# Decoder block on one Trainium2 core: where and in what pieces three layer-norm statistics are taken, the term order of the first two projections, and the spacing of the feed-forward transposes

## The chip, the cores and the metric

The kernel runs on one core of one Trainium2 chip. The metric is the device time of one execution in microseconds, the median of several. The engines are PE (TensorE, matmuls and transposes), DVE (VectorE), ACT (ScalarE), POOL (GpSimd) and SP (SyncE, which only issues transfers). Each works through its own list of instructions in order, and they wait for each other by semaphores.

## The reference: what is computed

`x` and `ctx` have 4 batches of 512 tokens by 512 features. Cut to what matters:

```
x = x + attn(layernorm(x), q_w, q_b, k_w, k_b, v_w, v_b, o_w, o_b)   # causal, 16 heads of 32
x = x + xattn(layernorm(x), ctx, ctx)                                # causal, 16 heads, no weights
h = layernorm(x)
x = x + relu(h @ W_up.T) @ W_down.T + sum(top-2 softmax of h @ W_gate.T) * (h @ W_expert)
```

Each layer norm takes mean and variance over the 512 features of a token, so there are three of them for each batch: before self-attention, before cross-attention and before the feed-forward.

## The kernel before, in words

**Work in steps and slots.** Both attentions are cut into 64 pairs of heads (32 groups of 4 heads). `ORDER` puts them in a row: 14 groups of self-attention, then `cscscc`, then 12 of cross-attention, so the groups 14, 16, 18, 19 are the four cross groups of batch 0, and 20 to 23, 24 to 27, 28 to 31 those of batches 1 to 3. A step `s` is one pair, and a slot `i` (0 to 7) is one of its 2 heads by 4 query blocks; `z = 8 * s + i`. I write slot 31.1 for step 31, slot 1. All engines walk the same steps, each with its own list.

**What a slot holds.** PE (loop at L652) does the scores of pair s+1 for slot i (`scores`, L466), then a quarter of a filler job, then the transposes of the probabilities of pair s (`turn`, L480). At slot 0 of even steps it also does probabilities times values of the group that ended (`values`, L513, called pv below), and at slot 1 of odd steps ahead of a cross group the queries' transposes (`queries`, L617). Scores have 3 PSUM banks: those of slot i wait until DVE is through the slot three before (L464). DVE (loop at L858) reduces the scores to a row maximum and moves them to `probs` (`top_of`, L682), copies the turned blocks 2, 3, 6, 7 (`turned`, L692), and takes reciprocals (L696), low halves of split operands (L768, L777, L804), the residual behind the output projection (L784), statistics (`ln_stats` L709 and L711, `f_stats_of` L716 and L718) and norms (L737, L745). ACT does the exponentials (L910), the other copies of turned blocks (L919) and the high halves. POOL scales the probabilities of self-attention (`scaled`, L1023, once DVE's reciprocal is there), adds a cross group's output to the residual (`added`, L1066, in step 2G+3 of group G), splits the keys (`keys`, L1056 and L1058) and the feed-forward weights (`f_split`, L1081 and L1083), and turns variances into reciprocal deviations (`ln_scale` L1034, `f_scale` L1040).

**Fillers.** `plan()` (L136) gives each projection its slots and one of two PSUM banks (`m_bank`): Q, K, V, the output projection O, and for the feed-forward of batch f from slot `feed_start(f)` = 344, 408, 472, 536: FL (4 transposes of the normed input, at u+1, u+2, u+4, u+5; the third waits until ACT and DVE have emptied the bank of the first), FG (gate), FU, FE, FD (up, expert, down). `plan()` also gives turns a free filler bank where one stands idle for long enough. Most projections are made of three products (`three`, L517): low times high, high times low, high times high, for each of 4 chunks of the contraction.

**Statistics before.** `stats_slots(j)`: j = 1 to 3 are the self-attention norms of batches 1 to 3. j = 4 to 7 are the cross-attention norms of batches 0 to 3: at slots 168, 169, 176, 177 (step 21 and 22), 256, 256, 272, 272 (steps 32 and 34), 339 to 342 (step 42), and 384, 384, 385, 385 (step 48). Batches 0 to 2 are read from the copy that SP loads back from memory (`load_x`, at steps 20, 30 and 40); batch 3 is read from `xres`. `f_stats_slots(f)`: slots 1, 2, 4, 5 of steps 41, 49, 57, 65, one token block of 512 features in each, after all four cross groups of the batch have been added.

**Start.** The first transposes go into `m0`, `m1`, `pv` and `t0`. The first projections Q0 and K0 run chunk by chunk, so their first product waits for the first low half (L750).

The statistics of before are

```python
            def f_stats_of(f, t):
                if t == 0:
                    dve.wait_ge(c_out, KC * (f + 1))
                nc.vector.bn_stats(f_stats[:, t, :], RES[f][:, t, :]).then_inc(f_stat, 1)
                dve.wait_ge(f_stat, NT * f + t + 1)
                nc.vector.bn_aggr(f_mv[:, t, :], f_stats[:, t, :]).then_inc(f_mv_done, 1)
```

and POOL's add, on which they wait, is the last thing but the scale factors in its step:

```python
                if s % 2 == 1 and other((s - 3) // 2):
                    added((s - 3) // 2)
```

## Time and profile before

| | |
|---|---|
| median of 3 runs | 714.7 us (713.9 to 716.91) |
| the profiled execution | 711.97 us, of which the span of its instructions is 710.0 us |
| PE busy | 674.7 us, 95% of the span |
| DVE, ACT, POOL busy | 70%, 71%, 36% |
| mean granted clock of TensorE | 0.995 |
| chain of work that ended last | PE 80%, DVE 7%, ACT 6% |

The profile is one execution; its own time is 711.97 us, 2.7 us under the median of the runs. A time in the trace is counted from the start of its span. A row of the timeline gives the start, the duration, the engine, the line, the operation with output and inputs, how many such instructions it merges, and in brackets how long the engine was idle just before and what released it. The granted clock is a share of 2.4 GHz, so 0.5 is 1.2 GHz.

### The profile page before, as it was taken

To read this page: it belongs to the slowest core of one execution; us is meant where nothing else is said; L and a number is where in the kernel's file an instruction comes from. 1 tells how busy PE (TensorE), PEld (TensorE's weight loads), DVE (VectorE), ACT (ScalarE), POOL (GpSimd) and SP (SyncE) were. 2 spreads that over 40 slices of the span, in tenths; PEclk is the share of its full clock that TensorE was granted. 3 is DMA by queue.
4 is the path that set the end of the run, shared out by engine and by line. 5 is a ranking of instruction groups with operands and counts; after the bars stand their busy time and mean duration, and the time that the engine had idled before them with its cause. 6 is when DMAs were issued, how large, how long until landed. Compare 5 with 4: busy or idle time off the path is not lost.

```text
span 710.0 us, 13884 instructions
## 1 busy us (share of the span) xinstructions
PE 674.7 (95%) x4488; PEld 523.8 (74%) x4488; DVE 494.6 (70%) x1730; ACT 501.4 (71%) x1450; POOL 256.9 (36%) x391
## 2 busy tenths in 40 slices
PE   7998999999999999999889987999989999899998
PEld 6777777777787777777666755777768777677786
DVE  6568766766766776776878788767887669664632
ACT  5678877777876778787899887776588667874110
POOL 4745644333555335742564415333112102000100
PEclk9999999999999999999999999999999999999999
DMA  9763533336423573445946584633463443510101
GB/s 313 186 155 75 141 70 90 82 94 185 116 61 90 124 212 84 102 105 146 275 122 168 153 236 121 166 95 97 96 183 89 111 101 87 163 38 1 59 1 59
DMA packets 52327, 86.12 MB, mean 121 GB/s; under 512 B 8609, under 2 KB 16801, under 8 KB 52257
## 3 DMA queue, kind: packets, MB, share of 16 engines
q1 hardware_dynamic: 52256, 85.25, 46.1%
q8 instruction: 36, 0.59, 0.3%
q14 instruction: 35, 0.28, 0.1%
HBM read 27.55 MB, written 7.34 MB: 49 GB/s over the span
## 4 chain that ended last, share of the span: by engine, by line
PE 80%; DVE 7%; ACT 6%; issue 2%; DMA 2%; POOL 2%; SPq 1%; POOLq 0%; ACTq 0%; DVEq 0%
PE t L480 16%; PE m L519 14%; PE m L520 14%; PE m L521 14%; PE pv L513 9%; PE s L466 8%; DVE probs L682 3%; ACT probs L910 3%; ACT prob L919 1%; PE m L585 1%; DVE prob L692 1%; DMA stack<-stage 1%; POOL probs L1023 1%; PE m L480 1%; PE m L534 1%
## 5 line engine op out<-in xcount | busy, mean ns | idle before, releaser
L682 DVE CUSTOM_DVE_ANT_0 probs<-s,mask 128x128 f32<-128x128 f32 (+3 forms) x512 | 246.6, 483 | 130.7 <-PE s L466 129.0
L910 ACT ACTIVATE probs<-probs,negmax 128x128 f32<-128x128 f32 (+3 forms) x512 | 284.5, 559 | 46.1 <-DVE negmax L682 45.2
L480 PE MATMUL t<-ident,probs 128*128 128x128 f32 x1140 | 203.5, 277 | 11.4 <-ACT prob L919 6.5
L466 PE MATMUL s<-stack 96*128 96x128 f32 (+3 forms) x512 | 197.8, 394 | 5.5 <-DVE negmax L682 2.8
L1023 POOL TENSOR_SCALAR probs<-probs,rsum 128x128 f32<-128x128 f32 (+3 forms) x256 | 133.4, 539 | 176.9 <-DVE rsum L696 176.6
L919 ACT ACTIVATE prob<-t 128x384 f32<-128x384 f32 (+1 forms) x231 | 124.7, 540 | 97.7 <-PE t L480 96.7
L480 PEld LDWEIGHTS t<-ident,probs 128*128 128x128 f32 x1140 | 144.7, 141 | 60.6 <-ACT prob L919 10.5
L466 PEld LDWEIGHTS s<-stack 96*128 96x128 f32 x512 | 97.9, 191 | 18.7 <-DVE negmax L682 4.1
L910 ACT ACTIVATION_READ_ACCUMULATOR probs<-probs,negmax 128x1 f32 x512 | 98.9, 193 | 0.0
L692 DVE COPY prob<-t 128x256 f32<-128x256 f32 (+1 forms) x218 | 77.1, 354 | 30.9 <-PE t L480 29.9
L519 PE MATMUL m<-xT_hi,w_lo 128*128 128x512 f32 x192 | 78.3, 408 | 1.2 <-DVE xT_lo L750 1.2
L520 PE MATMUL m<-xT_lo,w_hi 128*128 128x512 f32 x192 | 75.7, 394 | 0.0
L521 PE MATMUL m<-xT_hi,w_hi 128*128 128x512 f32 x192 | 75.5, 393 | 0.0
L519 PE MATMUL m<-w_hi,xT_lo 128*128 128x512 f32 x128 | 52.7, 412 | 0.0
L520 PE MATMUL m<-w_lo,xT_hi 128*128 128x512 f32 x128 | 50.4, 394 | 0.0
L521 PE MATMUL m<-w_hi,xT_hi 128*128 128x512 f32 x128 | 50.2, 392 | 0.0
L682 DVE DVE_READ_ACCUMULATOR2_ANT negmax<- 128x1 f32 x512 | 42.5, 83 | 0.0
L521 PEld LDWEIGHTS m<-xT_hi,w_hi 128*128 128x128 f32 x192 | 36.1, 188 | 8.6
L513 PE MATMUL pv<-prob,cv 128*32 128x128 f32 (+3 forms) x512 | 38.0, 436 | 1.5 <-ACT prob L919 1.4
L519 PEld LDWEIGHTS m<-xT_hi,w_lo 128*128 128x128 f32 x192 | 36.7, 191 | 2.8 <-DVE xT_lo L750 1.4
L520 PEld LDWEIGHTS m<-xT_lo,w_hi 128*128 128x128 f32 x192 | 36.5, 190 | 2.9
L513 PE MATMUL pv<-prob,V 128*32 128x128 f32 (+3 forms) x512 | 37.8, 435 | 0.1
(144 smaller groups left out, 946.2 us busy)
## 6 DMA issues: line engine op xcount, KB each, us to landing
stack<-stage SPq DMA_DIRECT2D x384, 128.0 KB, 2.3
xt<-in_x SPq DMA_DIRECT2D x16, 256.0 KB, 4.7
xres<-in_x SPq DMA_DIRECT2D x4, 1024.0 KB, 6.1
kraw<-in_ctxT SPq DMA_DIRECT2D x16, 256.0 KB, 3.0
cv<-in_ctx SPq DMA_DIRECT2D x16, 256.0 KB, 3.1
x<-xres SPq DMA_DIRECT2D x3, 1024.0 KB, 5.5
res<-x SPq DMA_DIRECT2D x8, 256.0 KB, 6.4
out<-res SPq DMA_DIRECT2D x2, 1024.0 KB, 4.8
```

The source lines that it names most:

```text
L466: nc.tensor.matmul(score_tile(P, i), stack[0:RS, P % 2, h, 0, chunk(qb)], stack[0:RS, P % 2, h, 1, 0:N], start=True, stop=True).then_inc(s ...
L480: mm = nc.tensor.transpose(dst[:, chunk(qb - kb)], probs[:, (2 * P + h) % 3, OFF[qb] + PART * kb:OFF[qb] + PART * kb + PART], ident[:, :])
L513: mm = nc.tensor.matmul(pv_bank[HD * j:HD * j + HD, PART * kb:T], v[:, HD * j:HD * j + HD], prob[kb][:, j, :], start=(kb == 0), stop=(kb = ...
L519: nc.tensor.matmul(dst, lhs[1], rhs[0], start=(c == 0), stop=False)
L520: nc.tensor.matmul(dst, lhs[0], rhs[1], start=False, stop=False)
L521: return nc.tensor.matmul(dst, lhs[0], rhs[0], start=False, stop=(c == KC - 1))
L534: mm = nc.tensor.transpose(dst[:, chunk(t)], src[:, t, chunk(c)], ident[:, :])
L682: nc.vector.tensor_tensor_reduce(probs[:, (2 * P + h) % 3, OFF[qb]:OFF[qb + 1]], score_tile(P, i), mask[:, T - N:T], -SCALE, BIG, ALU.add, ...
L692: nc.vector.tensor_copy(prob[kb][:, 2 * (P % 2) + h, :], turned_tile(P, i)).then_inc(t_dve, 1)
L910: nc.scalar.activation(tile, tile, ACT.Exp, bias=negmax[:, P % 2, h, qb:qb + 1], scale=-1.0, accum_out=total).then_inc(p_exp, 1)
L919: nc.scalar.activation(prob[kb][:, 2 * (P % 2) + h, :], turned_tile(P, i), ACT.Copy).then_inc(t_act, 1)
L1023: nc.gpsimd.tensor_scalar(tile, tile, rsum[:, P % 2, h, qb:qb + 1], 0.0, ALU.mult, ALU.add).then_inc(p_done, 1)
```

## The change

It does five things.

1. The statistics of cross-attention for batches 0 to 2 are taken from `xres`, one slot after the output projection's residual of the same token block is there (steps 10 to 12, 18 to 20, and 25, 28, 29, 30), with their own buffers for each batch and their own scale step on POOL (`c_scale`, steps 12, 20, 30, 48). The norm itself stays where it was, and now waits for the loaded copy. SP waits for these statistics before it overwrites `xres`. Batch 3 keeps its slots.
2. The statistics of the feed-forward are taken for each cross group when it has been added: in slots 1, 2, 4, 5 of step 2G+3 of every cross group G (steps 31, 35, 39, 41, 43, 45 and so on to 65), 128 features for each of 4 token blocks, so 64 narrow statistics in place of 16 wide ones; behind the fourth group they are aggregated.
3. Q0 and K0 do the four products of high parts first, and the others behind them.
4. The first transposes go into the three score banks and `pv`.
5. The third and fourth transposes of FL move one slot back (u+5 and u+6), for batches 0 to 2.

```diff
-def stats_slots(j):
+def o_start(b, t):
+    if b == B - 1:
+        return PAIRS * (SELF_END + min(t, 2)) + 4 * (t // 3)
+    if b == B - 2:
+        return PAIRS * (25, 28, 29, 29)[t] + 4 * (t // 3)
+    return PAIRS * (PAIRS * (b + 1) + 1 + t) + (4, 4, 0, 1)[t]
...
+def c_stats_slots(b):
+    z = PAIRS * PAIRS * (2 * B - 2)
+    return [z, z, z + 1, z + 1] if b == B - 1 else [o_start(b, t) + NT + 1 for t in range(NT)]
...
-def f_stats_slots(f):
-    z = PAIRS * (PAIRS * (f + B + 1) + 1)
+def f_stats_slots(G):
+    z = PAIRS * (2 * G + 3)
     return [z + 1, z + 2, z + 4, z + 5]
...
             if f < B - 1:
-                put(("FL", f, m), 0, u + 1 + m + m // 2, 1, 1)
+                put(("FL", f, m), 0, u + 1 + m + 2 * (m // 2), 1, 1)
...
-        first_bank = [*m_bank, pv_bank, t_bank[0]]
+        first_bank = [*s_bank, pv_bank]
...
                     sp.wait_ge(x2_stored[b - 1], 16)
+                    sp.wait_ge(c_mv_done, NT * b)
                     sp.dma_start(xres[:, :, :], x_in[b]).then_inc(res_loaded, 16)
...
+            def first_three(dst, w, k):
+                late = ([("lo", c) for c in (0, 1)] + [("x", c) for c in range(KC)] + [("lo", c) for c in (2, 3)] if w == WQ else
+                        [("x", c) for c in range(KC)] + [("lo", c) for c in range(KC)])
+                terms = [("hi", c) for c in range(KC)] + late
+                for n in range(3 * k, 3 * k + 3):
...
+            def c_stats_of(b, t):
+                dve.wait_ge(o_out, NT * b + t + 1)
+                nc.vector.bn_stats(c_stats[:, t, :], xres[:, t, :]).then_inc(c_stat, 1)
+                dve.wait_ge(c_stat, NT * b + t + 1)
+                nc.vector.bn_aggr(c_mv[:, b, t, :], c_stats[:, t, :]).then_inc(c_mv_done, 1)
+            def f_stats_of(G, t):
+                n = RANK[G]
+                f = n // KC
+                dve.wait_ge(c_out, n + 1)
+                nc.vector.bn_stats(f_stats[:, t, n % KC, :], RES[f][:, t, chunk(n % KC)]).then_inc(f_stat, 1)
+                if n % KC == KC - 1:
+                    dve.wait_ge(f_stat, NT * n + t + 1)
+                    nc.vector.bn_aggr(f_mv[:, t, :], f_stats[:, t, :, :].rearrange("p c s -> p (c s)")).then_inc(f_mv_done, 1)
...
+            def c_norm(b, t):
+                if t == 0:
+                    dve.wait_ge(c_rstd_done, b + 1)
...
+                if b < B - 1:
+                    dve.wait_ge(x_loaded[t], 16 * (B + b + 1))
...
+                for j in range(B):
+                    if s == c_stats_slots(j)[-1] // PAIRS:
+                        c_scale(j)
                 for f in range(B):
-                    if s == f_stats_slots(f)[-1] // PAIRS:
+                    if s == f_stats_slots(CROSS_AT[KC * f + KC - 1])[-1] // PAIRS:
                         f_scale(f)
```

## Rows read from the trace of the kernel before

**Rows 1.** The page, part 1: busy time and share of the span.

```profile
PE 674.7 (95%) x4488; PEld 523.8 (74%) x4488; DVE 494.6 (70%) x1730; ACT 501.4 (71%) x1450; POOL 256.9 (36%) x391
```

**Rows 2.** Groups by line, DVE: busy us, mean ns of one; idle before.

```profile
L709 DVE BATCH_NORM_STATS2 stats<-xt 128x6 f32<-128x512 f32 x20 | 13.6, 679 | 4.3 <-DMA xt<-in_x 4.3
...
L711 DVE BATCH_NORM_AGGREGATE mv<-stats 128x2 f32<-128x6 f32 x32 | 5.8, 182 | 1.1
```

**Rows 3.** Busy time in stretches of 10 us: PE, PEld, DVE, ACT, POOL, clock, DMA.

```profile
200.00:210.00 10.00, 10.00 (x59) 8.29 (x58) 7.21 (x29) 8.04 (x23) 6.59 (x11) 1.00 0.35 80
...
430.00:440.00 10.00, 6.22 (x38) 4.90 (x37) 8.44 (x31) 7.96 (x27) 4.39 (x6) 0.91 0.58 146
```

**Rows 4.** Timeline, the start: the last high half, Q0's first and twelfth product.

```profile
12.07 0.62 ACT L979 ACTIVATE xT_hi<-t 128x512 fp32r<-128x512 f32 x1
...
12.15 0.47 PE L519 MATMUL m<-xT_hi,w_lo 128*128 128x512 f32 x1 [1.24 <-DVE xT_lo L750]
...
14.77 0.39 PE L521 MATMUL m<-xT_hi,w_hi 128*128 128x512 f32 x1
```

**Rows 5.** Timeline of step 31, DVE, POOL and PE.

```profile
342.98 0.18 DVE L696 RECIPROCAL rsum<-rowsum 128x4 f32<-128x4 f32 x1
...
343.25 2.06 POOL L1023 TENSOR_SCALAR probs<-probs,rsum 128x128 f32<-128x128 f32 x4 [1.66 <-DVE rsum L696]
...
343.56 0.56 DVE L682 CUSTOM_DVE_ANT_0 probs<-s,mask 128x384 f32<-128x384 f32 x1 [0.41 <-PE s L466]
...
345.28 1.28 POOL L1066 TENSOR_TENSOR xt<-cn,xt 128x512 f32<-128x512 f32 x1
...
345.76 0.36 PE L466 MATMUL s<-stack 96*128 96x256 f32 x1
...
347.64 2.36 PE L513 MATMUL pv<-prob,V 128*32 128x512 f32 x32
```

**Rows 6.** Timeline of step 35, DVE, POOL and PE.

```profile
373.83 0.56 DVE L682 CUSTOM_DVE_ANT_0 probs<-s,mask 128x384 f32<-128x384 f32 x1 [0.42 <-PE s L466]
...
375.68 1.28 POOL L1066 TENSOR_TENSOR xt<-cn,xt 128x512 f32<-128x512 f32 x1
...
376.61 0.69 DVE L804 TENSOR_TENSOR stage<-pv,stage 128x512 fp32r<-128x512 f32 x1
...
377.40 2.36 PE L513 MATMUL pv<-prob,V 128*32 128x512 f32 x32
```

**Rows 7.** Timeline of steps 41 to 43, PE and POOL.

```profile
425.35 0.33 PE L466 MATMUL s<-stack 96*128 96x128 f32 x1 [1.03 <-DMA stack<-stage]
...
431.22 1.28 POOL L1058 TENSOR_TENSOR stage<-kraw,stage 128x512 fp32r<-128x512 f32 x1
...
437.33 0.23 POOL L1034 TENSOR_SCALAR veps<-mv 128x4 f32<-128x4 f32 x1 [4.84 <-DVE mv L711]
...
438.08 0.90 PE L480 MATMUL t<-ident,probs 128*128 128x128 f32 x3 [1.11 <-DVE prob L692]
...
438.65 0.61 POOL L1081 CAST w_hi<-V 128x512 fp32r<-128x512 f32 x1
...
442.49 1.27 POOL L1066 TENSOR_TENSOR res<-cn,res 128x512 f32<-128x512 f32 x1
...
443.36 0.66 PE L534 MATMUL m<-ident,f_xln 128*128 128x128 f32 x4 [1.42 <-DVE xT_lo L768]
...
447.78 2.36 PE L513 MATMUL pv<-prob,cv 128*32 128x512 f32 x32
```

**Rows 8.** Timeline of step 51, PE: FL's third transposes, the next pv.

```profile
525.59 0.66 PE L534 MATMUL m<-ident,f_xln 128*128 128x128 f32 x4 [1.51 <-DVE xT_lo L768]
...
530.00 2.36 PE L513 MATMUL pv<-prob,cv 128*32 128x512 f32 x32
```

**Rows 9.** Timeline at the end of step 11, PE and DVE.

```profile
151.90 2.36 PE L513 MATMUL pv<-prob,V 128*32 128x512 f32 x32
...
153.17 0.29 DVE L692 COPY prob<-t 128x128 f32<-128x128 f32 x1
```

More of the change, by code:

```diff
@@ L273, in decoder_block @@
         rstd = sb("rstd", [PART, NT])
-        f_stats = sb("f_stats", [PART, NT, 6])
+        c_stats = sb("c_stats", [PART, NT, 6])
+        c_mv = sb("c_mv", [PART, B, NT, 2])
+        c_veps = sb("c_veps", [PART, B, NT])
+        c_rstd = sb("c_rstd", [PART, B, NT])
+        f_stats = sb("f_stats", [PART, NT, KC, 6])
         f_mv = sb("f_mv", [PART, NT, 2])
@@ L521, in three @@
                 return nc.tensor.matmul(dst, lhs[0], rhs[0], start=False, stop=(c == KC - 1))
+            def first_three(dst, w, k):
[3 more added lines that the diff above has]
+                for n in range(3 * k, 3 * k + 3):
+                    term, c = terms[n]
+                    if term == "hi":
+                        pe.wait_ge(w_hi_done[w], c + 1)
+                        pe.wait_ge(lnt_hi, c + 1)
+                    elif term == "x":
+                        pe.wait_ge(lnt_lo, c + 1)
+                    elif w == WQ and c >= 2:
+                        pe.wait_ge(wq_rest, c - 1)
+                    else:
+                        pe.wait_ge(w_lo_done[w], c + 1)
+                    weight = w_lo if term == "lo" else w_hi
+                    mm = nc.tensor.matmul(dst, weight[:, w, c, chunk(0)], (xT_lo if term == "x" else xT_hi)[:, c, :],
+                                          start=(n == 0), stop=(n == 3 * KC - 1))
+                return mm
             def bank_for(key):
@@ L549, in fill @@
                     w = WQ if kind == "Q" else WK
-                    if n == 0 and kind == "Q" and c >= 2:
-                        pe.wait_ge(wq_rest, c - 1)
-                    elif n == 0:
-                        pe.wait_ge(w_lo_done[w], c + 1)
-                    if kind == "Q" and n % KC == 0:
-                        pe.wait_ge(lnt_lo, KC * (n // KC) + c + 1)
-                    mm = three(dst, (w_hi[:, w, c, chunk(n % KC)], w_lo[:, w, c, chunk(n % KC)]),
-                               (xT_hi[:, c, :], xT_lo[:, c, :]), c)
+                    if kind == "Q" and n and n % KC == 0:
+                        pe.wait_ge(lnt_lo, KC * (n // KC) + c + 1)
+                    if n == 0:
+                        mm = first_three(dst, w, c)
+                    else:
+                        mm = three(dst, (w_hi[:, w, c, chunk(n % KC)], w_lo[:, w, c, chunk(n % KC)]),
+                                   (xT_hi[:, c, :], xT_lo[:, c, :]), c)
                     if c == KC - 1:
@@ L883, in _ @@
                         back_scaled(s // 2 - 1)
-                    for j in range(1, 2 * B):
+                    for j in range(1, B):
                         for t in range(NT):
@@ L887, in _ @@
                                 ln_stats(j, t)
+                    for j in range(B):
+                        for t in range(NT):
+                            if z == c_stats_slots(j)[t]:
+                                c_stats_of(j, t)
+                    for j in range(1, 2 * B):
                         for t in range(NT):
                             if z == norm_slots(j)[t]:
-                                ln_norm(j, t)
+                                ln_norm(j, t) if j < B else c_norm(j - B, t)
+                    for G in CROSS_AT:
+                        for t in range(NT):
+                            if z == f_stats_slots(G)[t]:
+                                f_stats_of(G, t)
                     for f in range(B):
-                        for t in range(NT):
-                            if z == f_stats_slots(f)[t]:
-                                f_stats_of(f, t)
                         for t in range(NT):
@@ L1122, in _ @@
                     added((s - 3) // 2)
-                for j in range(1, 2 * B):
+                for j in range(1, B):
                     if s == stats_slots(j)[-1] // PAIRS:
                         ln_scale(j)
+                for j in range(B):
+                    if s == c_stats_slots(j)[-1] // PAIRS:
+                        c_scale(j)
                 for f in range(B):
-                    if s == f_stats_slots(f)[-1] // PAIRS:
+                    if s == f_stats_slots(CROSS_AT[KC * f + KC - 1])[-1] // PAIRS:
                         f_scale(f)
```

65 lines of the change are left out of this document (25 added, 40 removed).

## The prediction

> **What bounds the kernel now.** I read the page's busy times first. PE is busy for 674.7 of 710.0 us [rows 1], so only some 35 us can be had by removing waits, and work moved to another engine helps only where PE stands idle for it. The busy time by stretch says where that is. From 200 to 210 us PE is busy throughout while DVE has 2.8 us to spare; from 430 to 440 us PE is busy for 6.22 us, DVE for 8.44, and the granted clock is 0.91 [rows 3], so for some 1.8 us of it PE ran at 1.2 GHz instead of 2.4. Then I read the timeline there and at the steps in which the change puts a new wait. So the sum is made at six places: the start, the new statistics under a full PE, steps 31 and 35, steps 41 to 43, and steps 51 and 59.
>
> **Start: -0.2 us.** Q0's first product starts at 12.15 us, behind 1.24 us of waiting for a low half [rows 4]. Products of high parts can start about 1 us earlier, but the fourth of them needs the last high half, which ends at 12.69 (12.07 + 0.62) [rows 4], and 9 of the 12 products are then still to start. The twelfth starts at 14.77, so they follow each other at (14.77 - 12.15) / 11 = 0.24 us, and 0.23 without the slower first one: 12.75 + 8 x 0.23 = 14.59 for the last start, against 14.77 [rows 4]. What follows (stage, transfer, first scores) is a chain behind it and moves along. Bounds: 0 and -1.2, the whole wait; I take the value that is worked out.
>
> **Cross statistics behind the output projection: +1.0 us.** 12 statistics of 0.68 us with 12 aggregates of 0.18 [rows 2], some 0.8 each as they overlap, move to steps 10 to 30. There PE is full and DVE is not [rows 3], so most cost nothing: the cover is DVE's idle time. Gone, it would cost up to 12 x 0.86 = 10 us. One slot in each batch is tight: in step 11 DVE takes the new one (slot 5) with two low halves of transposes beside it, and its last copy of the step ends at 153.46, while pv, begun at 151.90, needs that copy for its last tenth, 0.9 x 2.36 = 2.1 us after its start, at 154.0 [rows 9]. 0.8 us more is 0.3 us too late. I count 0.3 for each of batches 0 and 1 and 0.4 for batch 2, whose steps 28 and 29 look the same. Range 0 to 2.4. What the old places give back: steps 21, 22 nothing (PE full); steps 32 and 34 nothing, since DVE did them in the shadow of a pv of 2.36 us [rows 5] and waited for the next scores behind them. SP's new wait and POOL's moved scale factors (two small instructions, the first 0.23 us [rows 7]) are met before they are due; in step 30 POOL has 1.66 us free ahead of 343.25 [rows 5], enough. Only step 42 gives something, below.
>
> **The feed-forward statistics, step 31: +3.0 us.** This is the new wait. In slot 31.1 DVE now waits for group 14 to be added. POOL does that add behind four scalings that wait for DVE's reciprocal of the same slot: reciprocal at 342.98, scalings 343.25 to 345.31, add 345.28 to 346.56 [rows 5]. DVE has nothing to do in between, as its list is in order; behind the wait stand all its maxima and copies. With a narrow statistic at 0.29, the price of DVE's 128-wide copy [rows 9] (bounds: 0.17, a quarter of a wide one, and 0.68, a whole one [rows 2]), the next maximum starts at 346.9 instead of 343.56, 3.3 us late. PE may run three slots of scores ahead: its scores of 32.5 were issued at 345.76 and need this maximum, so PE stops there. Before the next pv DVE has to do two more narrow statistics (0.6) and has some 0.9 us of its own old waits (0.41 of them in the row of 343.56) to absorb them: 3.3 + 0.6 - 0.9 = 3.0, pv at 350.6 instead of 347.64 [rows 5]. Nothing gives it back, as ACT has work without a pause from there to step 34. Bounds: 1.5 (about the wait from 345.76 to the end of that maximum, 346.9 + 0.56 - 0.1 = 347.4, alone) and 4.7 (see the clock, next).
>
> The clock could add to this. The row first: in the one stretch of 10 us in which PE stood idle for 3.8 us, in pieces of at most 1.11 us [rows 7], the granted clock was 0.91 [rows 3], that is 0.09 x 10 / 0.5 = 1.8 us at 1.2 GHz; so short waits, close together, have lowered it in this kernel. The Trainium skill has a rule that speaks against new waits of this kind: "TensorE: Matmul & The Clock Gate", section on psum-queue depth-cycling, says that PE idling briefly between groups of matmuls makes the clock oscillate, and that what is lost between the bursts is the price; the trace agrees. By the rule each of steps 31 and 35 would carry a slow spell and the sum would be 3.4 us more. I leave it out of the sum, since PE idles less in these two steps than from 430 to 440, and make it rival B, whose price comes from rows.
>
> **Step 35: +3.1 us.** The same again: group 16 is added behind the scalings of step 35, and that add ends at 376.96. The maximum behind it stood at 373.83, and comes at 377.2, 3.4 us late; the low half of the queries at 376.61 comes at 379.9, and pv waits for it: 380.5 instead of 377.40 [rows 6]. POOL's scale factor that was in the way here is gone, but the reciprocal decides. Bounds 1.5 and 4.8. From step 37 on no scalings stand before the add, which then ends before DVE arrives.
>
> **Steps 41 to 43: -4.4 us.** Step 41 has four wide statistics less and narrow ones instead (-1.9 us of DVE). I give it nothing: the first scores of the next pair wait for a transfer until 425.35 [rows 7], and DVE's earlier end meets the same transfer. Step 42 loses four statistics (-3.3 us), and here DVE was last: PE's waits for DVE include 1.11 us at 438.08 [rows 7]. With 3.3 less, ACT is last, and the step ends 3.0 us earlier. In step 43 there is a new wait: group 20 is added at 442.49 [rows 7]. POOL stood there for 4.84 us for the statistics of step 42, and then split two chunks (438.65 to 442.49, 3.84 us). Without that wait the splits start behind the keys at 432.5 and end at 436.35, and the add at 437.6; DVE, by my count, arrives at 435.4, so it loses 2.2 us. FL's third transposes now come a slot later, so their wait of 1.42 us [rows 7] overlaps PE's own work. Following slot by slot, I get pv at 443.2 instead of 447.78, -4.6 us, and take 0.2 off for copies that share POOL's and DVE's time. Bounds -6.5 (no wait for POOL) and -2.5 (PE at 1.2 GHz once more).
>
> **Steps 51 and 59: -2.4 us.** FL's third transposes waited 1.51 us at 525.59 for the low half of the first [rows 8]. That half is ready no earlier after the change, but the scores and turns of one slot (0.6 us) now run before, ACT's copies of those turns come earlier, and the last turn of the step no longer waits for one: pv at 528.8 instead of 530.00 [rows 8], -1.2 each. Bounds -0.5 and -1.5 each. Batch 3 has no FL in `plan()`. The narrow statistics of the other odd steps (4 x 0.29 on DVE in a step in which PE is full) have room: 0, at most 2 in all.
>
> Sum: -0.2 + 1.0 + 3.0 + 3.1 - 4.4 - 2.4 = +0.1 us. Against the profiled execution, 711.97 us, this is 712.1; the median of the runs stands 2.7 us above it, and I add the same: 714.8. A small allowance for the narrow statistics of the other steps, 0.4, makes **715.2 us**.
>
> **The rivals.** *A, the waits in 31 and 35 cost little, faster.* It needs PE's lookahead to cover them. Against it: PE is three score slots ahead at most. For it: ACT and PE had small waits in the same steps. At 0.8 each instead of 3.0 and 3.1, the time is 715.2 - 4.5 = 710.7, and with step 43's wait gone too 709.
>
> *B, the clock falls behind the new waits, slower.* Place: behind slots 31.5 and 35.5, and again in step 43. For it: the row above, and the new waits put about 3 us of idle time into 4.5 us twice. Against it: PE's idle time before them is less. Price: the spell of 430 to 440 goes on into the next stretch about as long, so 3.5 us at half speed, which puts off 1.7 us of PE's work. It decides the sign as soon as two of the three places carry such a spell. Two spells make 715.2 + 3.4 = 718.6, three 720.3.
>
> *C, the transposes' move does nothing*, since the low half is ready at the same moment: +2.4 and 1 us of step 43, 718.6.
>
> **How the numbers follow.** My forecast, gains and new waits that cancel, has 0.5. A has 0.22, B 0.2, C 0.08. The bounds of step 31, 35 and 41 to 43 together are about +-4, so the range is 710.0 to 719.5. Half a per cent is 3.6 us, about what a measurement of this kernel can tell from no change: under 711.1 is A, over 718.3 is B and C.
>
> **What would show it.** DVE idle for about 3.4 us in slots 31.1 and 35.1, released by POOL's add; the pv behind each 3 us later against the step's start; step 42 shorter by 3 us, no wait of FL at step 51 above 1 us; PE busy about the same in total. I am wrong if DVE's waits for the add are under 1 us, if step 42 is as long as before (ACT last), or if the granted clock is at 0.5 in steps 31 to 36.

## The result: slower by 1.6 per cent, outside the range

The changed kernel takes 727.7 us in the median of 4 runs (721.79 to 729.19), the kernel before 715.2 beside it (713.9 to 716.91). The ratio is 1.016, 95% interval 1.010 to 1.022. Forecast were 715.2 us and a range up to 719.5, so the result is slower than any case that I gave weight to. The profiled execution took 729.19 us, its span 727.2, with a mean granted clock of 0.983 (before: 0.995).

The page of the changed kernel, part 1, answers to [rows 1]:

```profile
PE 685.3 (94%) x4488; PEld 524.6 (72%) x4488; DVE 496.4 (68%) x1778; ACT 501.3 (69%) x1450; POOL 258.0 (35%) x391
```

PE does the same 4488 instructions in 10.6 us more of busy time. Work has not grown, so the instructions themselves were slower. Most of that is the clock. By my estimate from the mean granted clocks, PE ran at half speed for (1 - 0.983) x 727.2 / 0.5 = 24.7 us instead of (1 - 0.995) x 710.0 / 0.5 = 7.1, and 17.6 us more at half speed put off up to 8.8 us of work. The rest of the 17.2 us of span, 6.6, is idle time. VectorE's total grew by 1.8 us; the groups by line answer to [rows 2]:

```profile
L734 DVE BATCH_NORM_STATS2 stats<-xt 128x6 f32<-128x512 f32 x16 | 10.9, 678 | 4.8 <-DMA xt<-in_x 4.8
L741 DVE BATCH_NORM_STATS2 c_stats<-xres 128x6 f32<-128x512 f32 x16 | 10.7, 670 | 0.0
...
L750 DVE BATCH_NORM_STATS2 f_stats<-res 128x6 f32<-128x128 f32 x32 | 9.1, 284 | 2.2 <-POOL res L1120 2.2
...
L750 DVE BATCH_NORM_STATS2 f_stats<-xt 128x6 f32<-128x128 f32 x16 | 4.6, 287 | 6.9 <-POOL xt L1120 6.9
```

In these groups a narrow statistic takes 284 and 287 ns, against the 290 that I estimated. The last column is the news: DVE stood 6.9 us for POOL's adds of batch 0 and 2.2 us for one later.

Busy time in stretches, which answers to [rows 3] (PE, PEld, DVE, ACT, POOL, granted clock, DMA):

```profile
200.00:210.00 10.00, 10.00 (x59) 8.24 (x58) 7.03 (x26) 8.32 (x25) 7.36 (x13) 1.00 0.35 79
...
430.00:440.00 10.00, 7.49 (x54) 5.21 (x56) 9.65 (x41) 9.92 (x33) 2.56 (x3) 1.00 1.07 309
440.00:450.00 10.00, 8.96 (x72) 6.54 (x65) 7.06 (x27) 6.48 (x21) 4.53 (x6) 0.83 0.67 150
```

Early on PE is as full as before. The crowded stage comes 13 us later (the scores that wait for a transfer start at 438.77 instead of 425.35 [rows 7]) and has its slow clock behind 440.

Where in time it was lost shows when the spans are cut into steps, each from the start of DVE's first maximum of a step to that of the next (from the timelines of the two kernels; steps not listed differ by less than 0.3 us, or, as 49 with 50, cancel):

| step | before | after | | step | before | after |
|---|---|---|---|---|---|---|
| 11 to 13 | 32.47 | 33.20 | | 41 to 43 | 28.78 | 26.58 |
| 19 to 21 | 32.48 | 33.17 | | 44 | 11.28 | 14.31 |
| 28 | 9.53 | 10.31 | | 51 | 8.89 | 8.29 |
| 31 | 6.58 | 9.60 | | 52 | 11.28 | 12.70 |
| 32 | 6.92 | 9.45 | | 59 | 8.90 | 8.30 |
| 35 | 6.83 | 10.02 | | 60 | 11.28 | 14.37 |
| 36 | 7.39 | 9.31 | | | | |

Steps 31, 32, 35 and 36 lose 10.7 us, steps 44, 52 and 60 lose 7.5, and only 41 to 43, 51 and 59 gain, 3.4 in all. First step 31 in the timeline of the changed kernel, POOL, DVE and PE, which answers to [rows 5]; the number in brackets is the idle time before an instruction and who ended it:

```profile
345.29 0.18 DVE L725 RECIPROCAL rsum<-rowsum 128x4 f32<-128x4 f32 x1
...
345.57 2.07 POOL L1071 TENSOR_SCALAR probs<-probs,rsum 128x128 f32<-128x128 f32 x4 [0.32 <-DVE rsum L725]
...
347.60 1.28 POOL L1120 TENSOR_TENSOR xt<-cn,xt 128x512 f32<-128x512 f32 x1
...
348.91 0.29 DVE L750 BATCH_NORM_STATS2 f_stats<-xt 128x6 f32<-128x128 f32 x1 [3.44 <-POOL xt L1120]
...
349.72 0.39 PE L477 MATMUL s<-stack 96*128 96x256 f32 x1 [1.39 <-DVE negmax L711]
...
352.98 2.58 PE L524 MATMUL pv<-prob,V 128*32 128x512 f32 x12
354.69 2.79 PE L524 MATMUL pv<-prob,V 128*32 128x384 f32 x24
```

DVE waits 3.44 us for the add, about what the prediction has, and PE stops three slots of scores later. But the weighted sum, 2.36 us before [rows 5], now takes 4.5 (352.98 to 354.69 + 2.79). The busy time by stretch, with the granted clock behind the POOL column, says why; a clock of 0.50 is 1.2 GHz where 1.00 is 2.4:

```profile
348.00:350.00 2.00, 0.61 (x4) 0.27 (x2) 1.09 (x5) 0.30 (x1) 1.27 (x2) 1.00 1.01 322
350.00:351.00 1.00, 0.75 (x5) 0.46 (x4) 1.00 (x6) 1.00 (x4) 0.92 (x2) 1.00 0.96 303
351.00:352.00 1.00, 0.93 (x4) 0.43 (x4) 1.00 (x7) 1.00 (x3) 0.63 (x2) 0.71 0.23 69
352.00:354.00 2.00, 1.53 (x10) 0.76 (x14) 2.00 (x8) 2.00 (x9) 2.00 (x2) 0.50 0.17 38
354.00:356.00 2.00, 2.00 (x20) 0.46 (x16) 0.43 (x5) 0.02 (x1) 0.66 (x2) 0.50 0.95 215
```

PE was busy for 0.61 us of the two before 350, and from some point between 351 and 352 on the clock is down. I call such a stretch a slow spell. Step 35 is the same picture (DVE's wait 3.42 us at 384.73; [rows 6]): from 380 to 390 the clock is 0.78 in the changed kernel and was 1.00 before.

The second loss stands in steps 44, 52 and 60. The rows are those of step 51 and the head of step 52, PE and DVE, and answer to [rows 8]:

```profile
539.71 0.66 PE L564 MATMUL m<-ident,f_xln 128*128 128x128 f32 x4 [0.82 <-DVE xT_lo L810]
...
543.33 0.68 DVE L810 TENSOR_TENSOR xT_lo<-m,xT_hi 128x512 fp32r<-128x512 f32 x1
544.06 0.73 PE L614 MATMUL m<-xT_hi,g_both 128*128 128x512 f32 x2 [1.90 <-DVE xT_lo L810]
...
544.72 2.36 PE L524 MATMUL pv<-prob,cv 128*32 128x512 f32 x32
```

FL's third transposes wait 0.82 us instead of 1.51, as forecast. But the gate's product (L614), which stands in PE's queue ahead of pv, now waits 1.90 us. It writes the bank that the third transposes filled, and that bank is free only when DVE has made its low half, at 543.33 + 0.68. In the kernel before, no such wait stands there. Measured from the start of step 51 (521.71 before, 535.63 after), pv starts 8.29 us in before the change and 9.09 behind it, 0.8 later instead of 1.2 earlier. No slow spell follows here, although PE was busy for only 0.16 of the two microseconds before 544:

```profile
542.00:544.00 2.00, 0.16 (x2) 0.02 (x1) 2.00 (x8) 2.00 (x7) 0.00 (x0) 1.00 0.54 120
544.00:546.00 2.00, 1.94 (x18) 0.79 (x22) 1.73 (x6) 0.14 (x2) 0.00 (x0) 1.00 0.88 199
```

So a wait of this kind can bring a slow spell and need not.

In steps 41 to 43, rows that answer to [rows 7]:

```profile
438.77 0.33 PE L477 MATMUL s<-stack 96*128 96x128 f32 x1 [2.06 <-DMA stack<-stage]
...
452.31 0.29 DVE L750 BATCH_NORM_STATS2 f_stats<-res 128x6 f32<-128x128 f32 x1 [2.17 <-POOL res L1120]
...
459.41 0.74 PE L614 MATMUL m<-xT_hi,g_both 128*128 128x512 f32 x2 [2.13 <-DVE xT_lo L810]
...
460.08 3.98 PE L524 MATMUL pv<-prob,cv 128*32 128x512 f32 x32
```

Last, step 11, which answers to [rows 9]; pv, begun at 151.98, stops for the late copy:

```profile
154.03 0.28 DVE L721 COPY prob<-t 128x128 f32<-128x128 f32 x1
...
154.47 0.43 PE L524 MATMUL pv<-prob,V 128*32 128x128 f32 x8 [0.35 <-DVE prob L721]
```

### The profile page after: what moved, and what is told of

It reads as the page before. It is cut to its first block, busy times and chain, and to the rows that moved or that the text cites. A ratio compares the mean times of both kernels' runs of the same rounds, so it can differ in the third digit from the quotient of the medians.

```text
span 727.2 us, 13938 instructions
## 1 busy us (share of the span) xinstructions
PE 685.3 (94%) x4488; PEld 524.6 (72%) x4488; DVE 496.4 (68%) x1778; ACT 501.3 (69%) x1450; POOL 258.0 (35%) x391
## 4 chain that ended last, share of the span: by engine, by line
PE 77%; DVE 8%; ACT 4%; DMA 3%; POOL 3%; issue 2%; SPq 2%; POOLq 0%; ACTq 0%
PE t L491 14%; PE m L530 14%; PE m L531 13%; PE m L532 13%; PE pv L524 10%; PE s L477 8%; DVE probs L711 3%; DMA stack<-stage 2%; ACT probs L958 2%; PE m L614 1%; POOL probs L1071 1%; DVE prob L721 1%; PE m L491 1%; SPq L389 1%; DVE xT_lo L810 1%
## 5 line engine op out<-in xcount | busy, mean ns | idle before, releaser
L491 PE MATMUL t<-ident,probs 128*128 128x128 f32 x1140 | 203.9, 277 | 11.3 <-ACT prob L967 5.6
L530 PE MATMUL m<-xT_hi,w_lo 128*128 128x512 f32 x184 | 75.1, 408 | 0.0
L531 PE MATMUL m<-xT_lo,w_hi 128*128 128x512 f32 x184 | 72.6, 395 | 0.0
L532 PE MATMUL m<-xT_hi,w_hi 128*128 128x512 f32 x184 | 72.3, 393 | 0.0
L524 PE MATMUL pv<-prob,cv 128*32 128x128 f32 (+3 forms) x512 | 42.1, 475 | 1.4 <-ACT prob L967 1.4
L524 PE MATMUL pv<-prob,V 128*32 128x128 f32 (+3 forms) x512 | 42.2, 472 | 0.7 <-DVE prob L721 0.7
L532 PEld LDWEIGHTS m<-xT_hi,w_hi 128*128 128x128 f32 x184 | 34.6, 188 | 8.2
L531 PEld LDWEIGHTS m<-xT_lo,w_hi 128*128 128x128 f32 x184 | 35.0, 190 | 2.7
L524 PEld LDWEIGHTS pv<-prob,cv 128*32 128x32 f32 x512 | 16.3, 117 | 27.6 <-issue 24.3
```

The lines of the kernel that those rows point to most:

```text
L491: mm = nc.tensor.transpose(dst[:, chunk(qb - kb)], probs[:, (2 * P + h) % 3, OFF[qb] + PART * kb:OFF[qb] + PART * kb + PART], ident[:, :])
L524: mm = nc.tensor.matmul(pv_bank[HD * j:HD * j + HD, PART * kb:T], v[:, HD * j:HD * j + HD], prob[kb][:, j, :], start=(kb == 0), stop=(kb = ...
L530: nc.tensor.matmul(dst, lhs[1], rhs[0], start=(c == 0), stop=False)
L531: nc.tensor.matmul(dst, lhs[0], rhs[1], start=False, stop=False)
L532: return nc.tensor.matmul(dst, lhs[0], rhs[0], start=False, stop=(c == KC - 1))
```

## The experiments

The theory after this profile: the narrow statistics cost by DVE's wait for the add, and once more by the clock behind it; the transposes' move hands its wait to the gate's product through a bank of PSUM. Rivals: narrow statistics cost by their number; the clock falls for another reason; the gate's product is held by its data or by DVE's queue, not by a bank.

### Each part of the change alone

Four kernels, each the kernel before with one part of the change; of each the lines that matter most are shown. Cross statistics behind the output projection:

```diff
-                    for j in range(1, 2 * B):
+                    for j in range(1, B):
                         for t in range(NT):
                             if z == stats_slots(j)[t]:
                                 ln_stats(j, t)
+                    for j in range(B):
+                        for t in range(NT):
+                            if z == c_stats_slots(j)[t]:
+                                c_stats_of(j, t)
```

> The kernel before with the cross statistics behind the output projection alone. Theory W: 0.75 us more in each of steps 11, 19 and 0.9 in steps 25 to 30, 2.3 us in all, and step 42 shorter by 3 us or more as DVE was last there, with a spell at 1.2 GHz behind steps 42 and 43 gone (1.5 us): 1 to 3 us less than before, 712 to 714 us. Rival: ACT or the transfer of step 42 takes over at once, step 42 shorter by under 1 us, and the time is 1 to 2 us above before, 716 to 717 us.

Feed-forward statistics by groups:

```diff
-    z = PAIRS * (PAIRS * (f + B + 1) + 1)
+    z = PAIRS * (2 * G + 3)
     return [z + 1, z + 2, z + 4, z + 5]
```

> The kernel before with the narrow feed-forward statistics alone. Theory W (DVE waits for POOL's add in steps 31 and 35, and TensorE's clock falls to 1.2 GHz behind the wait): DVE idle 3.4 us in 31.1 and again in 35.1, steps 31 and 35 3 us longer each, steps 32 and 36 2 us longer each by the clock, step 41 at most 1 us shorter; 7 to 10 us more than before, 722 to 725 us. Rival N (the 48 more instructions on DVE cost, wherever they stand): 0.3 to 0.5 us more in each odd cross step and none in particular in 31 and 35, 718 to 721 us. My prediction's size without the clock: about 6 us, 721 us.

Transposes further apart:

```diff
-                put(("FL", f, m), 0, u + 1 + m + m // 2, 1, 1)
+                put(("FL", f, m), 0, u + 1 + m + 2 * (m // 2), 1, 1)
```

> The kernel before with the transposes FL at u+1, 2, 5, 6 alone. Theory B (the gate product FG takes the bank of the third transposes and waits until DVE has its low half, so the wait only moves on, and is longer than the one removed): steps 43, 51, 59 shorter by 0.6 us, steps 44, 52, 60 longer by 1.4 us or more, 3 x 0.8 = 2.4 us more than before without and up to 7 us more with the clock at 1.2 GHz behind each wait; 717.5 to 722 us. Rival P (my prediction's step): 1.2 us less in each, 711.5 us.

First projections over high parts first, with the first transposes in the score banks:

```diff
-        first_bank = [*m_bank, pv_bank, t_bank[0]]
+        first_bank = [*s_bank, pv_bank]
```

> The kernel before with the start alone (high parts first, other banks). Theory: the first scores wait for the same chain of transfers, so the first maximum stands within 0.3 us of 25.11 us and the time is that of before, 715.2 us within 1. Rival (the first norm and transposes come later by their new banks, as the profile after has them at 8.73 in place of 8.19 us): 0.5 us later at the first maximum, 715.7 us.

Measured, beside the kernel before at 713.57 us:

| part alone | median us | ratio, 95% interval |
|---|---|---|
| cross statistics | 711.14 | 0.995, 0.993 to 0.998 |
| feed-forward statistics by groups | 728.45 | 1.020, 1.015 to 1.024 |
| transposes apart | 715.66 | 1.002, 1.000 to 1.005 |
| start | 713.94 | 1.001, 0.999 to 1.003 |

The start leaves the time as it was, as expected (its first maximum, at 24.57 us, is 0.5 earlier and not within 0.3 as I wrote). The cross statistics are 0.9 us better than their range (712 to 714), the narrow statistics 3.5 us worse than theirs (722 to 725), and the transposes 1.8 us below theirs (717.5 to 722). The product of the four ratios is 1.018, and the change has 1.016. By the medians the loss of the whole is that of the narrow statistics, and the other three parts about cancel.

The steps don't add up as the medians do. Alone, the narrow statistics have DVE waits of 3.42 and 3.57 us in steps 31 and 35, which take 9.58 and 10.14 us, as in the change. But steps 32 and 36 are 8.20 and 8.46 us, only 1.3 and 1.1 above the kernel before, with shorter slow spells behind the same waits. And step 43 is at 15.42 (before 10.44, change 9.77). The timeline of that kernel shows POOL's queue there:

```profile
444.76 0.23 POOL L1093 TENSOR_SCALAR c_veps<-c_mv 128x4 f32<-128x4 f32 x1 [4.83 <-DVE c_mv L748]
...
449.89 1.26 POOL L1125 TENSOR_TENSOR res<-cn,res 128x512 f32<-128x512 f32 x1
...
451.18 0.29 DVE L755 BATCH_NORM_STATS2 f_stats<-res 128x6 f32<-128x128 f32 x1 [5.18 <-POOL res L1125]
...
453.93 1.12 PE L565 MATMUL m<-ident,f_xln 128*128 128x128 f32 x4 [4.32 <-DVE xT_lo L815]
```

POOL waits for the cross statistics that are still in step 42, then splits weights, then adds, and DVE waits for that. A slow spell adds to it, the longest of any profile here:

```profile
446.00:458.00 12.00, 7.68 (x35) 7.16 (x35) 4.97 (x19) 5.79 (x17) 8.64 (x10) 0.50 0.00 0
```

How the 5 us of step 43 divide between wait and clock no run shows. Cross statistics taken early remove most of the wait, 5.18 against 2.17 us. Alone the cross statistics are the best part: steps 41 to 43 fall from 28.78 to 25.21 us, for 2.2 us paid in steps 11 to 28.

### The narrow statistics one step later

```diff
 def f_stats_slots(G):
-    z = PAIRS * (2 * G + 3)
+    z = PAIRS * (2 * G + 3 + (RANK[G] % KC < KC - 1))
```

> The changed kernel with one edit: VectorE takes the narrow statistics of a group one step later, except for the last group of each batch, so that in steps 31 and 35 it no longer stands before GpSimd's addition. Theory 1 (VectorE's in-order wait, and TensorE's clock falling behind it): both the wait and the slow step behind it go. Steps 31, 32, 35, 36 fall from 9.60, 9.45, 10.02, 9.31 to about 6.8, 7.3, 6.9, 7.6 us, the granted clock stays at 1.0 there, and the time is 717 (715 to 719). Rival (waits alone, the clock falls for another reason): steps 31 and 35 fall but 32 and 36 stay above 9 us, 721.5. Rival (narrow statistics cost by their number, not by their place): the time stays above 724.

Measured: 713.43 us, ratio to before 0.999 (0.998 to 1.000). That is 14.3 us less than the change by the medians, and some 12 by the two ratios. Steps 31, 32, 35, 36 are 6.61, 7.53, 6.70 and 8.16 us, and steps 33 and 37 give back 1.4 more. The windows of the two stretches, clock 1.00:

```profile
350.00:360.00 10.00, 8.97 (x78) 6.28 (x70) 8.12 (x36) 8.56 (x30) 3.96 (x4) 1.00 0.83 204
380.00:390.00 10.00, 9.22 (x76) 6.83 (x69) 9.07 (x37) 8.90 (x29) 1.89 (x2) 1.00 0.74 183
```

The number of narrow statistics is the same, 64, so the rival that they cost by their number falls: it is the place. It came out below the range of my expectation (715 to 719); of the 15.8 us of span between the two profiled executions, 10.8 lie in steps 31 to 37, and the rest mostly in steps 41 to 43 (2.1) and 60 (1.7, the clock). This edit takes wait and slow clock away together, and can't part them.

### PE kept busy through the wait of step 31

```diff
+                    if s == 31 and i in (4, 6):
+                        left(14)
+                        for _ in range(6 if i == 4 else 2):
+                            nc.tensor.matmul(pv_bank[:, :], w_hi[:, WQ, 0, chunk(0)], xT_hi[:, 0, :], start=True, stop=True)
```

> The changed kernel, with six 512-column matmuls whose result nobody reads put into TensorE's queue in slot 4 of step 31 and two in slot 6, in the bank of the weighted sum, which is free then: TensorE works through most of the time in which VectorE waits for the addition. Nothing is left out of the computation. Theory (the clock falls because TensorE stood idle): the wait of VectorE and step 31 stay (9.3 to 10.0 us), but the granted clock stays at or near 1.0 behind it and step 32 is back from 9.45 to about 7.0 us; the time is 725.3 (724 to 727, with the spells at step 36 and later still there). Rival (the clock falls for a reason that has nothing to do with the idle time): step 32 stays at 9.4 and the time at 727.7 or above.

Measured: 726.16 us (724.99 to 726.71), 1.6 us below the changed kernel, whose own runs reach down to 721.79. Timeline and windows of this kernel:

```profile
347.17 1.63 PE L696 MATMUL pv<-xT_hi,w_hi 128*128 128x512 f32 x6
...
348.00 0.29 DVE L754 BATCH_NORM_STATS2 f_stats<-xt 128x6 f32<-128x128 f32 x1 [3.45 <-POOL xt L1124]
...
351.88 2.36 PE L524 MATMUL pv<-prob,V 128*32 128x512 f32 x32
```

```profile
350.00:360.00 10.00, 8.69 (x73) 5.87 (x73) 8.45 (x36) 8.25 (x26) 2.73 (x3) 1.00 0.72 181
380.00:390.00 10.00, 7.89 (x48) 4.05 (x49) 6.38 (x25) 4.23 (x13) 1.07 (x1) 0.66 0.30 67
```

DVE's wait is the same 3.45 us and step 31 the same 9.63, but the clock stays at 1.00 from 350 to 360, pv is back at 2.36 us, and step 32 at 6.73 us instead of 9.45. In step 35, where nothing was filled in, the clock falls as in the change. So the wait costs 3.0 us by itself, and in this pair of profiles PE's idle time costs 2.7 more one step later, by the clock. It is one execution of each kernel, and a slow spell doesn't follow every such wait: step 52 has the same two waits in both kernels (0.82 and 1.90 us) and takes 12.70 us in the changed one and 14.33 here, and step 60, again with the same waits, takes 14.37 and 12.67. For the idle time as the cause speaks that both profiles with the wait of step 31 unfilled (the change, and the narrow statistics alone) have the spell and the filled one has not. What decides in a single case is open.

The Trainium skill names the effect ("TensorE: Matmul & The Clock Gate", section "A second HAM failure mode: psum-queue depth-cycling"): where TensorE idles briefly and often between groups of matmuls, the clock goes down and up, and throughput is lost to that. This pair of kernels agrees, with 2.7 us.

### Only the fourth transposes later

```diff
-                put(("FL", f, m), 0, u + 1 + m + m // 2, 1, 1)
+                put(("FL", f, m), 0, u + 1 + m + m // 2 + m // 3, 1, 1)
```

> The kernel before with only the fourth of the feed-forward's transposes one slot later, the third where it was. Theory (the first gate product waits for the bank that the third transposes leave, which VectorE's low part empties): the gate product finds its bank as before, no wait of over 0.6 us stands before it, steps 44, 52 and 60 stay at 11.3 us (they were 14.37, 12.68 and 14.30 when both were moved), and the time is 713.5 or up to 1 below the kernel before. Rival (any later transpose delays the product through its data): the product waits 1.3 to 1.8 us as when both were moved, and steps 44 and 60 are above 13 us, 715.5.

Measured: 714.01 us, ratio 1.000 (0.999 to 1.002). The timeline of steps 51 and 52, PE:

```profile
528.53 0.66 PE L565 MATMUL m<-ident,f_xln 128*128 128x128 f32 x4 [1.51 <-DVE xT_lo L816]
...
532.28 0.73 PE L616 MATMUL m<-xT_hi,g_both 128*128 128x512 f32 x2
...
532.94 2.25 PE L523 MATMUL pv<-prob,cv 128*32 128x512 f32 x28
```

The gate's product has no wait. With the third transposes moved too (the transposes alone) it waits 1.32 us for DVE's low half, at 531.80. Of these two only the third's bank is the one that the product takes over, and in its first slot the product reads only the high halves of the first two transposes (`fill`, kind FG). So it is the bank and not the data, and that rival falls. DVE's queue has a share in it: the low half that empties the bank stands in that queue. With the narrow statistics of step 51 ahead of it the wait is 1.90 us (the change), without them 1.32. Steps 44, 52 and 60 take 11.87 us, not 11.3 as expected, and steps 51 and 52 together 20.18 us, 20.17 before: this half of the move is worth nothing.

Step 42 took 13.55 us in this profile, against 10.22 before with the same work, at a clock of 0.55 from 424 to 430. The edit changes nothing ahead of step 43, so this is taken up in the last section.

### The gate's product behind the weighted sum

The transposes apart as in the change, alone on the kernel before, and

```diff
-GATE_AT, UP_AT, TURN_AT, EXP_AT, DOWN_AT, UNITS = 8, 12, 13, 28, 44, 60
+GATE_AT, UP_AT, TURN_AT, EXP_AT, DOWN_AT, UNITS = 9, 12, 14, 28, 44, 60
```

> The kernel before with the feed-forward's transposes further apart as in the change, and the first gate product one slot later, behind the weighted sum of step 44, 52 and 60 instead of ahead of it (the turn of the gate's logits one slot later with it). Theory (with the transposes moved, the first gate product waits for the bank that the third transposes leave, and the weighted sum waits behind it in TensorE's queue): the weighted sum no longer waits, the bank is free when the product comes, and the 1.2 us of the move are kept: steps 51 and 59 at 7.7 us, 52 and 60 at 11.3 instead of 12.7 and 14.3, no granted clock at 0.5 there, 711.5 (710.5 to 712.5) against 713.6 for before and 715.7 for the move alone. Rival (the product's data or VectorE's queue set the time, not its place): steps 52 and 60 stay above 12.5 us, 715 or more.

Measured: 715.22 us, ratio 1.002 (0.999 to 1.004). Half of the theory held and the number did not. Steps 51 and 52 are 7.71 and 10.72 us (expected 7.7 and 11.3). But steps 45, 53 and 61 are longer by 2.3, 2.1 and 2.1 us, with a new wait at the up projection:

```profile
542.43 0.50 PE L529 MATMUL m<-xT_hi,w_lo 128*128 128x512 f32 x1 [1.45 <-DVE w_lo L835]
```

The expectations of the later runs call this the bank of the turned gate. It isn't, as `plan()` of this kernel shows. With u the first slot of the feed-forward, the gate's product holds its bank one slot longer, until u+16. That is the slot in which the second up product starts, and the first up product's bank comes free in the same slot. `plan()` then gives the second up product the bank that the first one has only just left, where before it got the gate's. L835 is DVE's low half of the first up product's result. So the wait is new and made by the choice of bank, and not the old wait handed on.

### Better places for the cross statistics, and both together

```diff
-    return [z, z, z + 1, z + 1] if b == B - 1 else [o_start(b, t) + NT + 1 for t in range(NT)]
+    if b == B - 1:
+        return [z, z, z + 1, z + 1]
+    a = o_start(b, 0) + NT + 1
+    if b == B - 2:
+        return [a, PAIRS * 30 + 4, PAIRS * 30 + 5, PAIRS * 30 + 6]
+    y = PAIRS * (PAIRS * (b + 1) + 4)
+    return [a, y + 4, y + 6, y + PAIRS + 2]
```

> The cross statistics alone, as before measured at 711.14, with seven of their places moved: those of rows 1 to 3 of the first two batches into steps 12 and 13 (20 and 21) instead of steps 11 and 12 (19 and 20), and those of the third batch into step 30 instead of 28 to 30, where VectorE waits for scores behind the weighted sum for 2.6 us. Theory (the 0.8 us of steps 11, 19 and 28 come from statistics that stand in VectorE's queue before a copy for which the weighted sum waits): steps 11 and 19 are 13.3 again and 28 is 9.5, up to 0.7 us each time, 709.0 (708.3 to 710). Rival (the statistics cost their 0.6 us wherever they stand, since VectorE has no slack): the same 711.1.

Measured: 711.35 us, ratio 0.996 (0.993 to 0.998), no better than 711.14 and above the 709.0 (708.3 to 710) of my expectation. The edit moves nine places; the expectation counts seven. Steps 11 and 19 are 13.34 and 13.35 again, and steps 11 to 13 together 32.74, 0.3 us above the kernel before instead of 0.7; step 28 is back at 9.51; but step 30, where I had moved three, grew from 11.09 to 12.86. So the 2.6 us of DVE's idle time that I had counted on behind a weighted sum were no room for three statistics in slots 4 to 6.

> Cross statistics with their places moved as in the run before, and the feed-forward's transposes further apart with the first gate product one slot later; wide feed-forward statistics and the start as before the change. If both theories hold: 709.0 less 2.4 to 3.0 us, 706.5 (705.5 to 708). If only the places hold 709, if only the gate 708.5 to 709.5, if none 711 to 713.

Measured: 714.36 us, ratio 1.001 (0.999 to 1.003), slower than every case that I had named: the up projection's wait of 1.45 us at steps 45, 53 and 61 again, and step 30 again.

### Cross statistics with the late narrow ones

```diff
-                put(("FL", f, m), 0, u + 1 + m + 2 * (m // 2), 1, 1)
+                put(("FL", f, m), 0, u + 1 + m + m // 2, 1, 1)
```

on the kernel with late narrow statistics, the start of before with it.

> The kernel before with two parts of the change: the cross statistics taken from the residual behind the output projection, and the feed-forward's statistics by groups, but those of all groups but a batch's last one step later than in the change. The start and the spacing of the feed-forward's transposes are those of before. Against the cross statistics alone (711.14): if narrow statistics a step late are free, steps 51 and 59 get shorter by the 0.35 us by which each of four statistics is narrower, about 0.5 us each, and step 43 as well: 709.5 to 710.5. If the wait for the addition in step 43 costs what it saves: 711 to 712. If the narrow statistics delay the even steps: 713 or more.

Measured: 712.52 us, ratio 0.997 (0.995 to 0.999). That is 1.4 us behind the cross statistics alone, measured at another time against the same kernel before, with intervals that overlap (0.993 to 0.998 there). Steps 51 and 59 are 8.90 us, as before the change, so narrow statistics a step later gain nothing there.

### The best kernel of this study

Cross statistics early, with the new places for batches 0 and 1 only, wide feed-forward statistics, the old start, the transposes apart and the whole chain behind them one slot later:

```diff
-GATE_AT, UP_AT, TURN_AT, EXP_AT, DOWN_AT, UNITS = 8, 12, 13, 28, 44, 60
+GATE_AT, UP_AT, TURN_AT, EXP_AT, DOWN_AT, UNITS = 9, 13, 14, 29, 45, 61
```

> The cross statistics of the change with the places of the first two batches' rows 1 to 3 in steps 12 and 13 (20 and 21), the feed-forward's transposes further apart as in the change, and its whole chain behind them (gate, up, turn, expert, down) one slot later, the end of each feed-forward too. Narrow statistics and the new start are not in it. Theory (moving the transposes hands the wait from bank to bank: first to the gate product, then, with the gate moved alone, to the up product of steps 45, 53 and 61, which waits 1.45 us for the bank of the turned gate; moved together, no link waits): steps 51 and 52 are 7.7 and 10.7, step 53 about 8.9 (10.85 with the gate moved alone), 1.6 us saved in each of three feed-forwards, about 1 us given back by the later end, and 0.9 us saved by the places: 711.1 - 0.9 - 4.8 + 1.0 = 706.4 (705 to 708.5). Rival (each later product finds its bank late in turn, since VectorE empties them in its own order): steps 53 and 61 stay above 10 us or a further step grows, 710.5 or more.

Measured: 708.39 us (707.63 to 710.12), ratio 0.991 (0.989 to 0.994), faster than both kernels. The size is at the slow end of what I expected: steps 51 and 52 are 7.90 and 10.11 us, but 53 is 10.38, above the 10 us that I had named as the rival's sign, and step 50 grew by 1.3. Of 1.6 us for each feed-forward only 0.1 to 1.4 stayed (43 to 47: 1.4 against the cross statistics alone; 50 to 55: 0.5; 58 to 61: 0.1). What holds steps 50 and 53 is open. In this kernel the second up product has the gate's bank again, and no wait of 1.45 us stands before it.

## Why the prediction was wrong, point by point

**The failed step** is the sentence in which I left the clock out of the sum, "since PE idles less in these two steps than from 430 to 440". The mechanism and its price stood there, as rival B with 0.2, and the third of my signs of being wrong, a granted clock at 0.5 in steps 31 to 36, came true. The comparison was made over 10 us, where the idle time of a wait is diluted; in the two microseconds before 350, PE was busy for 0.61. That alone doesn't settle it either, as the windows from 542 to 546 show, so the spells could be given a chance and a price, but not be ruled out. Steps 32 and 36 lost 2.5 and 1.9 us by it, and the profile shows the clock down again at 441, 461 and 628. B's price of 1.7 was right for a spell like that of step 60: steps 52 and 60 of the changed kernel have the same two waits (0.82 and 1.90 us), and take 12.70 and 14.37 us, the one with the clock at 1.00 behind them, the other at 0.50 from 628 to 630. At step 32 it was too small (2.7), and in the kernel with the narrow statistics alone too large (1.3 and 1.1). Its count was too small: I had three places, and the changed kernel has five.

**Steps 31 and 35:** forecast +3.0 and +3.1, measured +3.02 and +3.19; DVE's waits were forecast at about 3.4 us and are 3.44 and 3.42. This part of the working held. Rival A falls.

**Steps 41 to 43, -4.4:** pv of step 44 came 0.8 us earlier against the start of step 41 instead of 4.6. The link with POOL was right (forecast wait 2.2, measured 2.17). Missing were the gate's product with 2.13 us, and a transfer that landed later: the scores waited 2.06 us instead of 1.03, and the clock fell behind that. Step 42 itself, forecast 3.0 us shorter, was 0.3 shorter (10.22 to 9.91); with the cross statistics alone it was 2.0 shorter (8.17), still not 3.0. The 1.9 us less of DVE in step 41 should read 1.6, 4 x (0.68 - 0.29); nothing hung on it.

**Steps 51 and 59, -2.4:** the second failed step. I followed the third transposes to pv slot by slot, but not the next owner of their bank, though the gate's product stands in the queue ahead of pv. Measured: 0.8 us for the worse at 51, 2.5 at 59 with 60, where the clock fell too. Rival C, "the transposes' move does nothing", comes nearest, and even it was too kind. The transposes alone do give step 51 the 1.2 us (7.71 against 8.89) and lose 1.4 in step 52 (12.68 against 11.28); in the change the narrow statistics take 0.6 more in step 51.

**Cross statistics, +1.0:** the copy was late by 0.35 us as worked out (0.3), but pv, once stopped, ended at 154.90 instead of 154.26 (151.90 + 2.36 [rows 9]), having begun 0.08 later, so stopping cost 0.2 on top. Mis-sized: 0.7 for each of batches 0 and 1, 0.8 for batch 2, 2.2 in all.

**Start, -0.2:** the change alone gives 1.001 (0.999 to 1.003), no difference that can be told. In the changed kernel the first product starts at 11.91 us instead of 12.15 [rows 4], but the last two of Q0 run from 15.06 to 15.68, so that the twelfth starts some 0.5 us later than the 14.77 of before instead of 0.2 earlier. What held them was not traced. DVE's first maximum stands at 25.20 instead of 25.11, and kernels with the old start have it anywhere from 24.04 to 25.45, so neither the gain nor this loss reaches the time.

**Narrow statistics of the other steps, +0.4:** too small. Alone they make steps 51 and 59 0.4 us longer each (9.29 against 8.89 and 8.90). In the changed kernel these steps take 8.29 and 8.30 us, and 7.71 with the narrow statistics one step later, so 0.6 each.

Taken together, the sum was made for 712.1 us and the profiled execution took 729.2. Of these 17.1 us the clock behind waits is 7.8 (steps 32 and 36 with 2.5 and 1.9, steps 44 and 60 with 1.7 each), steps 41 to 43 are 3.6 (4.4 less 0.8), the places of 51 and 59 are 4.0 (0.8 each instead of -1.2, without the clock), and the cross statistics 1.2. That is 16.6; the start and small differences are the rest.

## What to carry to other kernels

A statistic that an in-order engine takes as soon as its data could be there costs the whole wait for that data, and everything behind it; one step later the same 64 instructions cost nothing in the median. When a new wait makes TensorE idle, put a possible slow spell beside it in the sum, 1.1 to 2.7 us in these profiles, and widen the range by it; whether it comes can't be told from the wait alone. When a transpose or product is moved later, follow its bank to the next owner: here the wait moved from the third transposes to the gate's product. And when a program deals out the banks, print them after every edit: one slot more for the gate made two up products in a row share a bank.

## What the runs showed of the hardware that I had not expected

**A slow spell costs nothing where TensorE isn't last.** The kernel before has one itself: windows of two microseconds, the clock after the POOL column.

```profile
354.00:356.00 2.00, 0.96 (x6) 0.60 (x6) 2.00 (x9) 2.00 (x7) 0.00 (x0) 1.00 0.89 215
356.00:358.00 2.00, 2.00 (x12) 1.92 (x11) 0.54 (x4) 2.00 (x9) 0.00 (x0) 0.55 0.51 125
358.00:360.00 2.00, 2.00 (x11) 1.64 (x10) 1.85 (x8) 2.00 (x8) 0.00 (x0) 0.60 0.00 0
```

ACT is busy all the time there. The kernel with the transposes alone does the same work in these steps at a clock of 1.00:

```profile
356.00:358.00 2.00, 2.00 (x15) 1.65 (x14) 1.27 (x8) 2.00 (x8) 0.00 (x0) 1.00 0.52 120
```

Steps 32 and 33 take 6.92 and 8.15 us in both.

**The times of one kernel go with its mean clock.** With the transposes alone, ten runs lie between 712.37 us at a mean granted clock of 0.995 and 718.33 at 0.988; the changed kernel has 721.79 at 0.992 and 729.19 at 0.983. The same waits bring a slow spell in one execution and not in the next, as steps 52 and 60 of the changed kernel and of the one with step 31 filled show, each with waits of 0.82 and 1.90 us: 12.70 and 14.33 us for step 52, 14.37 and 12.67 for step 60.

**Step 42 varies most, and why is open.** The last wait of step 41, for the stack's transfer, is 0.87 us (cross statistics alone), 1.03 (before), 1.83 (best kernel), 2.06 (change) and 2.82 (step 31 filled). Step 42 goes from 8.17 us in the first to 10.30 in the best kernel, which do the same work there; the clock is 0.50 from 428 to 430 in both, and to 432 in the second. But the landing isn't all. With the gate's product behind the weighted sum that wait is 1.68 us, and step 42 takes 13.22 us against 10.22 before, at a clock of 0.50 from 424 to 430. That and the 13.55 us of the fourth transposes are the largest differences between profiles that do the same work in a step. So a total that moves by 2 or 3 us from one profile to the next need not come from the edit. What sets the landing was not tried.
